# One DMA for each x, cond, bias and output tile, new orders of the five engines in the loading phase, and base loaded ahead of the recurrent LSTM weights

## What is computed

```python
ys = cond / sqrt(512);  d = rsqrt((ys*ys) @ (w0*w0) + 1e-8)
x = x + ((x * ys) @ w0) * d                                  # L0
h = tanh(h @ Wh1 + x @ Wx1 + b1), h0 = cond;    x = x + h    # L1, a recurrence over 128 steps
xw = gelu(layernorm(cond) @ w1 + b1) @ w2 + b2               # L2: cond alone gives a low-rank
layer = base + A @ B^T (A, B: two halves of xw, rank 8)      #     matrix for each sequence
x = x + x + x @ layer^T
gates = x @ Wx3 + h @ Wh3 + b3                               # L3, an LSTM over 128 steps
c = f*c + i*g;  h = o*tanh(c);                  x = x + h
```

## Time and profile before

| what | us |
|---|---|
| median of 3 runs | 1211.31 (1210.25 to 1211.34) |
| the profiled execution | 1212.77 |
| its span in the trace | 1211.0 |
| PE, DVE, ACT, POOL busy | 1149.9, 858.9, 480.3, 56.0 |

### The profile page before, as it was taken

The page is one execution under the profiler, slowest core; times in us unless marked ns, Lnnn a source line. Parts: engine busy times, 40 slices in busy tenths (PEclk is TensorE's granted clock), DMA queues, the critical chain, the costliest instruction groups (busy, mean ns, idle before and its releaser), DMA issues.

```text
span 1211.0 us, 50535 instructions
## 1 busy us (share of the span) xinstructions
PE 1149.9 (95%) x22740; PEld 751.8 (62%) x22740; DVE 858.9 (71%) x2389; ACT 480.3 (40%) x1160; POOL 56.0 (5%) x75
## 2 busy tenths in 40 slices
PE   3885999999999999999999999999999999999985
PEld 1562666666666666666666666666666666666542
DVE  4796777777777777777777777777777777776553
ACT  4694333333333343333333433333334333334332
POOL 1000000000000000000000000000000000000000
PEclk9888999999999999999999999999999999999999
DMA  9982000000000000000000000000000000000000
GB/s 321 390 302 67 3 20 21 20 21 20 20 15 8 20 20 21 20 20 20 11 12 20 20 20 21 20 21 11 12 20 20 21 20 20 11 8 6 11 11 18
DMA packets 49064, 50.99 MB, mean 42 GB/s; under 512 B 5984, under 2 KB 38752, under 8 KB 47184
## 3 DMA queue, kind: packets, MB, share of 16 engines
q1 hardware_dynamic: 47984, 47.50, 12.5%
q10 hardware_dynamic: 864, 0.26, 0.1%
HBM read 39.36 MB, written 8.39 MB: 39 GB/s over the span
## 4 chain that ended last, share of the span: by engine, by line
PE 63%; DVE 19%; ACT 11%; issue 4%; DMA 2%; ACTq 0%; DVEq 0%
PE ps_gates L1331 20%; PE ps_gates L1323 18%; PE ps_x L1262 7%; PE ps_l L1262 6%; PE ps_rnn L1347 4%; PE ps_rnn L1350 3%; ACT rows L476 2%; PE ps_lr L1262 2%; DVE gates_ring L998 2%; PE ps_z L1262 2%; DVE lstm_hT L1009 2%; ACT gates_ring L598 2%; DVE late L987 1%; DVE rnn_h L841 1%; ACT x L476 1%
## 5 line engine op out<-in xcount | busy, mean ns | idle before, releaser
L1331 PE MATMUL ps_gates<-big,lstm_h 128*32 128x512 f16 x6144 | 355.0, 380 | 9.9 <-ACT lstm_h L476 8.1
L1323 PE MATMUL ps_gates<-big,rows 128*32 128x512 f16 x6144 | 355.3, 380 | 3.5 <-DVE rows L742 3.5
L1323 PEld LDWEIGHTS ps_gates<-big,rows 128*32 128x32 f16 x6144 | 164.8, 97 | 171.8 <-issue 5.6
L1331 PEld LDWEIGHTS ps_gates<-big,lstm_h 128*32 128x32 f16 x6144 | 152.4, 96 | 163.4 <-ACT lstm_h L476 16.3
L998 DVE SCALAR_TENSOR_TENSOR gates_ring<-ps_gates,tile_un,rows 128x256 f32<-128x256 f32 x256 | 111.5, 477 | 42.0 <-PE ps_gates L1331 42.0
L598 ACT ACTIVATE gates_ring<-gates_ring 128x256 f32<-128x256 f32 x128 | 53.5, 418 | 199.7 <-DVE gates_ring L998 199.7
L1347 PEld LDWEIGHTS ps_rnn<-rnn_h,wh_hi 128*128 128x128 f16 x2048 | 90.4, 96 | 57.5 <-issue 52.6
L1347 PE MATMUL ps_rnn<-rnn_h,wh_hi 128*128 128x64 f16 x2048 | 120.5, 192 | 3.9 <-DVE rnn_h L841 3.9
L1350 PE MATMUL ps_rnn<-rnn_h,wh_lo 128*128 128x32 f16 x2048 | 116.1, 177 | 0.0
L476 ACT ACTIVATE lstm_h<-lstm_hT,tile_g 128x128 f16<-128x128 f32 x128 | 51.6, 403 | 120.4 <-DVE lstm_hT L1009 120.4
L1350 PEld LDWEIGHTS ps_rnn<-rnn_h,wh_lo 128*128 128x128 f16 x2048 | 90.8, 97 | 0.0
(11 more groups left out here) (180 smaller groups left out, 1552.2 us busy)
## 6 DMA issues: line engine op xcount, KB each, us to landing
ring<-in_hw SPq DMA_DIRECT2D x16, 1024.0 KB, 12.6
xT_sb<-in_xT SPq DMA_DIRECT2D x128, 64.0 KB, 2.3
outT<-late SPq DMA_DIRECT2D x128, 64.0 KB, 2.1
big<-in_wx SPq DMA_DIRECT2D x5, 1024.0 KB, 7.8
big<-in_wh SPq DMA_DIRECT2D x5, 1024.0 KB, 12.2
big<-in_w SPq DMA_DIRECT2D x1, 1024.0 KB, 5.8
big<-in_hw SPq DMA_DIRECT2D x1, 1024.0 KB, 11.8
late<-in_base SPq DMA_DIRECT2D x1, 1024.0 KB, 18.3
```

Of the source, the lines that this page charges most:

```text
L1323: nc.tensor.matmul(ps_gates[t % 2][B * j:B * j + B, :], x16[:, part, k, at:at + B], wx3_part(w_part, k)[:, GW * j:GW * j + GW], start=(n = ...
L1331: last = nc.tensor.matmul(ps_gates[t % 2][B * j:B * j + B, :], lstm_h16[:, part, k], wh3_part(w_part, k)[:, GW * j:GW * j + GW], start=Fal ...
```

## The change

1. x tiles, output tiles, condT and b1T are moved by one DMA each in place of four (`by_feature` in place of `by_block`). The partitions that hold the features stay the same. condT moves from ACT's queue to the head of SP's.
2. SP issues base behind blocks 4 to 7 of w2, ahead of the four parts of Wh3. The squares of base are taken before those of Wh3, and POOL's order follows.
3. The layer norm no longer waits for hb1T, which has a semaphore of its own.
4. The calls of the loading phase stand in another order on all five engines. ACT's tanh of a recurrence step and its `high` part may stand apart (`rnn_tanh`, `rnn_high`), and so may DVE's `x3_first` and `x3_low`. In the main loop the calls follow each other as before.

```diff
-        def by_block(x, j):
-            return x.rearrange("(f k) j n -> j f k n", k=KC)[j]
+        def by_feature(x):
+            return x.rearrange("(f k) j n -> j f k n", k=KC)
...
         def x_landed(engine, c):
-            engine.wait_ge(ld_x[c % XT_RING], 16 * KC * (c // XT_RING + 1))
+            engine.wait_ge(ld_x[c % XT_RING], 16 * (c // XT_RING + 1))
...
             def load_x(c):
-                for j in range(KC):
-                    sp.dma_start(xT_sb[c % XT_RING][FB * j:FB * j + FB].rearrange("p k t b -> p k (t b)"),
-                                 by_block(xT[c].rearrange("p j t b -> p j (t b)"), j)).then_inc(ld_x[c % XT_RING], 16)
+                sp.dma_start(xT_sb[c % XT_RING][:].rearrange("p k t b -> p k (t b)"),
+                             by_feature(xT[c].rearrange("p j t b -> p j (t b)"))).then_inc(ld_x[c % XT_RING], 16)
...
+            sp.dma_start(condT_sb[:], by_feature(condT)).then_inc(ld_cond, 16)
             load_weight(w0, W0_SLOT, ld_w0)
             load_x(0)
...
             for c in range(1, XT_RING):
                 load_x(c)
-            for j in range(KC):
-                sp.dma_start(b1T_sb[FB * j:FB * j + FB], b1T.rearrange("(f k) j -> j f k", k=KC)[j],
-                             allow_slow_non_contiguous=True).then_inc(ld_b1, 16)
+            sp.dma_start(b1T_sb[:], b1T.rearrange("(f k) j -> j f k", k=KC), allow_slow_non_contiguous=True).then_inc(ld_b1, 16)
             for k in range(KC):
                 sp.dma_start(wx3_staged(k), by_row(wx3)[:, k]).then_inc(ld_wx3[k], 16)
             for n in range(RING, 2 * RING):
                 sp.wait_ge(w2_used, n - RING + 1)
                 load_w2(n)
+            sp.dma_start(late[:].rearrange("p (k n) -> p k n", k=KC), by_row(base)).then_inc(ld_base, 16)
...
                 else:
                     sp.wait_ge(u_parts, 1)
                 sp.dma_start(wh3_staged(k), by_row(wh3)[:, k]).then_inc(ld_wh3[k], 16)
-            sp.dma_start(late[:].rearrange("p (k n) -> p k n", k=KC), by_row(base)).then_inc(ld_base, 16)
             for n in range(2 * RING, 4 * KC):
...
                 sp.wait_ge(out_ready, STEPS * (a + 1))
-                for j in range(KC):
-                    sp.dma_start(by_block(out[a].rearrange("p j t b -> p j (t b)"), j),
-                                 x3T[a % 2][FB * j:FB * j + FB].rearrange("p k t b -> p k (t b)"))\
-                      .then_inc(st_out[a % 2], 16)
+                sp.dma_start(by_feature(out[a].rearrange("p j t b -> p j (t b)")),
+                             x3T[a % 2].rearrange("p k t b -> p k (t b)")).then_inc(st_out[a % 2], 16)
             for q in range(2):
-                sp.wait_ge(st_out[q], 16 * KC * TILES // 2)
...
-            def rnn(r):
+            def rnn_tanh(r):
                 i, s = r // STEPS, r % STEPS
-                h = x2T[i % X2_RING][:, :, s]
                 act.wait_ge(rnn_pre_ready, r + 1)
                 if s == 0:
                     wait(act, x2_lo_ready, i - X2_RING + 1)
-                nc.scalar.activation(h, rnn_pre[:], ACT.Tanh).then_inc(rnn_h_ready, 1)
+                nc.scalar.activation(x2T[i % X2_RING][:, :, s], rnn_pre[:], ACT.Tanh).then_inc(rnn_h_ready, 1)
+
+            def rnn_high(r):
                 act.wait_ge(rnn_h_ready, r + 1)
-                high(rnn_h16[:, :, 0], h, s_h).then_inc(rnn_hi_ready, 1)
+                high(rnn_h16[:, :, 0], x2T[r // STEPS % X2_RING][:, :, r % STEPS], s_h).then_inc(rnn_hi_ready, 1)
+
+            def rnn(r):
+                rnn_tanh(r)
+                rnn_high(r)
 
...
-            for j in range(KC):
-                act.dma_start(condT_sb[FB * j:FB * j + FB], by_block(condT, j)).then_inc(ld_cond, 16)
             act.dma_start(ln_rows[:, 0], cond).then_inc(ld_rows, 16)
             act.dma_start(ln_rows[:, 1], ln_g.partition_broadcast(B)).then_inc(ld_rows, 16)
             act.dma_start(ln_rows[:, 2], ln_b.partition_broadcast(B)).then_inc(ld_rows, 16)
-            act.dma_start(hb1T_sb[:], hb1T).then_inc(ld_rows, 16)
-
+            act.dma_start(hb1T_sb[:], hb1T).then_inc(ld_hb1, 16)
+
+            act.wait_ge(ld_w0, 16)
+            squares(big[:, SQ_SLOT], big[:, W0_SLOT], 1)
             act.wait_ge(ln_var_ready, 1)
             nc.scalar.activation(ln_s[:, 1:2], ln_s[:, 0:1], ACT.Sqrt).then_inc(ln_root_ready, 1)
-            act.wait_ge(ld_w0, 16)
-            squares(big[:, SQ_SLOT], big[:, W0_SLOT], 1)
             act.wait_ge(ld_wx1, 16)
             unused_squares(big[:, WX1_SLOT], 2, 1)
...
+            rnn(5)
+
+            nc.scalar.activation(unused[:], s_h, ACT.Sigmoid)
+            copy_rows(2)
...
+            copy_rows(3)
+            rnn_tanh(7)
+            b_high()
             wh3_high(2, 0)
-            copy_rows(3)
             wh3_high(2, 1)
+            low_rank_share(0)
+            x3_high(0)
             wh3_high(3, 0)
-
-            nc.scalar.activation(unused[:], s_h, ACT.Sigmoid)
-            b_high()
...
-            def x3(a):
-                x3_flat = x3T[a % 2].rearrange("p k t b -> p (k t b)")
+            def x3_first(a):
                 dve.wait_ge(tile_un_ready, a + 1)
-                wait(dve, st_out[a % 2], 16 * KC * (a // 2))
+                wait(dve, st_out[a % 2], 16 * (a // 2))
                 dve.wait_ge(base_ps, a + 1)
                 dve.wait_ge(lr_ready, a + 1)
-                nc.vector.scalar_tensor_tensor(x3_flat, ps_x3[:], tile_un[:, a, 1:2], x3_lr, ALU.mult, ALU.add)\
-                  .then_inc(x3_ready, 1)
+                nc.vector.scalar_tensor_tensor(x3T[a % 2].rearrange("p k t b -> p (k t b)"), ps_x3[:], tile_un[:, a, 1:2], x3_lr,
+                                               ALU.mult, ALU.add).then_inc(x3_ready, 1)
+
+            def x3_low(a):
                 dve.wait_ge(x3_hi_ready, a + 1)
-                low(x3_16[a % 2][:, 1].rearrange("p k n -> p (k n)"), x3_flat, tile_g[:, a, 0:1],
-                    x3_16[a % 2][:, 0].rearrange("p k n -> p (k n)")).then_inc(x3_lo_ready, 1)
+                low(x3_16[a % 2][:, 1].rearrange("p k n -> p (k n)"), x3T[a % 2].rearrange("p k t b -> p (k t b)"),
+                    tile_g[:, a, 0:1], x3_16[a % 2][:, 0].rearrange("p k n -> p (k n)")).then_inc(x3_lo_ready, 1)
 
             def lstm_gates(t):
                 a, gates = t // STEPS, gates_sb[t % 2]
...
             nc.vector.tensor_scalar(ln_s[:, 0:1], moments[:, 1:2], LN_EPS, None, ALU.add).then_inc(ln_var_ready, 1)
             x_magnitude(0, 0)
+            xs(0)
...
+            wh1_low(0)
+            x_magnitude(1, 1)
             xs(1)
-            dve.wait_ge(ld_b1, 16 * KC)
+            x_magnitude(2, 2)
+            x_magnitude(3, 3)
+            x1_low(0)
...
             pe.wait_ge(folds_ready, 3)
+            pe.wait_ge(ys_ready, 2)
+            pe.wait_ge(sq_ready, 1)
+            folded_parts(ps_x3, ysq, w0_sq).then_inc(dsum_parts, 1)
             pe.wait_ge(ae_ready, 1)
             for k in range(KC):
...
             w2_unit(1)
             w2_unit(2)
+            w2_unit(3)
             pe.wait_ge(wx1_lo_ready, 2)
             l1(0)
-            w2_unit(3)
+            l0(1)
             pe.wait_ge(wh1_lo_ready, KC)
             pe.wait_ge(h0_lo, 1)
             rnn(0)
-            l0(1)
+            w2_unit(4)
             rnn(1)
-            w2_unit(4)
             w2_unit(5)
+            w2_unit(6)
             rnn(2)
+            w2_unit(7)
             l1(1)
+            turn_a()
             rnn(3)
-            w2_unit(6)
-            w2_unit(7)
             l0(2)
-            turn_a()
             rnn(4)
-            rnn(5)
-            l1(2)
             w2_unit(8)
             w2_unit(9)
+            rnn(5)
             w2_unit(10)
-            w2_unit(11)
             pe.wait_ge(a_lo_ready, 4)
             z(0)
+            w2_unit(11)
+            l1(2)
             rnn(6)
+            w2_unit(12)
+            w2_unit(13)
+            rnn(7)
+            w2_unit(14)
+            w2_unit(15)
+            move_b()
             pe.wait_ge(base_lo_ready, 2)
             x3_base(0, range(KC))
-            w2_unit(12)
-            w2_unit(13)
-            w2_unit(14)
-            rnn(7)
-            w2_unit(15)
-            move_b()
             pe.wait_ge(b_lo_ready, 2)
             x3_low_rank(0)
             pe.wait_ge(wx3_lo_ready, 2 * KC)
```

More of the change, by code:

```diff
@@ L660, in _ @@
+            wx3_high(2, 1)
+            copy_rows(1)
+            rnn(2)
+            base_squares()
+            wx3_high(3, 0)
+            wx3_high(3, 1)
+            rnn(3)
+            a_high()
             wh3_squares(0)
-            rnn(3)
-            copy_rows(1)
-            wx3_high(2, 0)
+            x2_high(0)
+            rnn(4)
+            base_high(0)
+            x1_high(2)
             wh3_squares(1)
             wh3_squares(2)
-            rnn(4)
-            x1_high(2)
             wh3_squares(3)
-            wx3_high(2, 1)
@@ L1058, in _ @@
             weight_scale(2, 3, wx1_scale_ready)
```

(82 more changed lines are left out.)

133 lines of the change are left out of this document (53 added, 80 removed).

## The result

| | before | after |
|---|---|---|
| time, median | 1210.78 us (1210.21 to 1211.34) | 1219.45 us (1218.12 to 1221.77) |
| profiled execution, its span | 1212.77, 1211.0 us | 1219.4, 1217.6 us |

The ratio is 1.0074, 95% interval 1.0056 to 1.0091: the change makes the kernel slower by 8.7 us. The forecast was 1218.9.

The account below looks back on a forecast made before the run. It took PE to bound the main loop and the last w2 block's landing plus a DMA-free chain the loading phase. Last block +6.8, chain -1.0 and tail +1.8 gave +7.6 on 1211.3: 1218.9 us, range 1202 to 1225.

Parts of the forecast that it names:

- Stall in the weight stream, -5.1: Loading phase: reordered w2 units free the four-place ring, removing the empty DMA stretch from 77.7 to 82.8 us; -5.1 us.
- Twelve x issues, -1.0: SP's queue in loading: three x issues in place of twelve stop the queue running dry; -1.0 us, bounds 0 and -2.
- The head, 0: Start of the kernel: earlier layer norm and one more ACT table load change nothing while DMAs set the pace; 0.
- Merging, +12.9: Loading phase: merged DMAs run over four engines and delay later weights; +12.9 us, bounds 0 and +17.
- condT's 1.6: Loading phase: condT's 128-byte packets on four engines cost 1.6 us more, the middle of 0 to 3.3.
- Last block, +6.8: End of the weight stream: the last w2 block lands at 104.1 us in place of 97.3, +6.8 us.
- Behind the last block, -1.0: Chain from the last w2 block to gates_x(0): b_high and b_low start earlier; -1.0 us, bounds +1.5 and -1.6.
- base ahead of Wh3, 0: Loading phase: base's DMA moved earlier arrives in time for DVE's base_diagonal; 0, bounds 0 and +2 us.
- Tail, +1.8: Kernel end: the single last output DMA over four engines lands later; +1.8 us, bounds -1.1 and +2.3.
- Sixteen engines: Rival for the merged DMAs: they are shared over all engines as before, -8.2 us, 1203.1 us; chance 0.22.
- Rival 2: Merged DMAs in between, as eight engines or cheaper packets: 1.1 us more a tile, 1206.8 us; chance 0.08.
- rival 3: Loading phase: late x tiles make DVE the bound, recurrence starting at 53 us, time 1219.7 us; chance 0.10.

Follow-up runs that it names:

- e1: The changed kernel with its new orders, but condT, x, b1T and output tiles each in four DMAs again: 1209.57 us, ratio 0.9999.
- e9: e1 with condT's four DMAs back at the head of ACT's queue: 1206.84 us, ratio 0.9963.
- e4: The changed kernel with x, cond, bias and output laid out by the host for one DMA each with 128 as outermost count: 1201.61 us, ratio 0.9933.
- e6: The kernel before, its orders kept, with the data layout and single DMAs of e4: 1206.43 us, ratio 0.9964.
- e2: The kernel before, its orders kept, with the merged DMAs alone: 1219.81 us, ratio 1.0088.
- e7: The changed kernel with x tiles alone in four DMAs again: 1211.92 us, ratio 1.0002.
- e8: e4 with GpSimd's product xs(3) moved ahead of its maximum of B: 1199.29 us, ratio 0.9896.
- e12: e8 with base's DMA moved back behind the four parts of Wh3: 1210.98 us, ratio 1.0002.

## Why the prediction came out, step by step

The time was right to 0.6 us and its main mechanism was right, but several sizes were wrong and cancelled, so that the number came out is in part luck. Of the signs that it named, the slow stretch came, but at 87 GB/s from 29 to 38 us where it had some 60 for 12; no stretch is empty ahead of the last block, PE waits 3.32 us for a DMA ahead of unit 8 and for DVE at most 0.8 us at a time on the way there, and the last block landed at 98.7, between its 104 and 91.

- **Stall in the weight stream, -5.1: right.** e1 against the kernel before moves 387 in place of 257 GB/s from 70 to 85 us: 1.95 MB or 5.0 us. At the last block the orders bring 4.3 us (e9) and, in the 128 form, 4.5 (e4 against e6).
- **Twelve x issues, -1.0: not had.** The ragged rates of the earlier trace rows were not a dry queue: the DMA share there is 1.25 from 28 to 30 us and 0.85 in the one us from 31. Three issues over four engines take SP longer than twelve. Only the 128 form has a gain, 407 (e4) against 340 GB/s (e1) from 27 to 42 us, or 2.6 us, and there fewer issues and longer runs are not told apart.
- **The head, 0: wrong.** condT's issues now stand ahead of all weights on SP. That costs e1 0.8 MB in the first 10 us, 2.1 us. Undoing it alone (e9) brings the last block 2.6 us earlier, the time by 4 us by the two ratios (2.3 between the profiled spans). The prediction weighed the layer norm's wait and the table load there, and put nothing down for what condT's place at the head of SP's list costs the weights behind it.
- **Merging, +12.9: mechanism right, size twice too large.** Measured 6.1 (after against e1) and 7.6 (e2 against before) at the last block, all of it by the x tiles (e7). I scaled a tile's time from 235 GB/s over sixteen engines to 59 over four, 4.5 us. Measured are 87 GB/s and 3.0 us. An engine of sixteen moves 15 GB/s of these packets and counts as fully busy (the share of 1.25), an engine of four moves 22. So the rate does not go with the number of engines; what the sixteen share that slows each packet was not tried. Of the 8.0 us that the stretch from 27 to 42 lost against e1 (207 GB/s over 15 us), 1.9 did not reach the last block (6.1 did), near the 2.3 taken. condT's 1.6 was nothing.
- **Last block, +6.8: measured +4.5**, as -4.3 from the orders (94.22 to 89.97), +2.6 from the head (to 92.61) and +6.1 from the merging (to 98.73).
- **Behind the last block, -1.0: measured +1.3, near its upper bound.** The earlier `b_low` is real: in e8 the chain is 12.45 us, 1.0 under 13.4. After the change, too, `b_low` starts 1.2 us behind the scale, where it was 2.3. But there two things cover it. `x3_low` took 1.76 us beside GpSimd's product; the prediction had not looked at GpSimd. And TensorE's granted clock was 0.50 (1.2 GHz) from 98.7 to 105.0, after PE had waited 2.15 us; unit 15 took 1.93 us there (1.07 before) and `move_b` 3.68. The wait alone doesn't decide it: in e8 PE had waited 2.19 us and the clock was 1.00. Nor does the program: `move_b` took 1.94 and 3.42 us in the two profiles of before. What decides was not found. Before, `move_b` at that clock (3.42 us in the second profile) lay beside the table load, and x3_base was done; now `x3_base(0)` stands behind it, and is on the path. Of the 2.2 us over e8's chain 1.0 is `x3_low`, 0.9 unit 15, and 0.3 `move_b` with `x3_base(0)` behind it, the rest of which lies beside DVE's own work. First `move_b` of before in the second profile and then the stretches: after the change, and in e8, where the clock is 1.00 (2.4 GHz):

```profile
96.00 3.42 PE L1254 MATMUL ps_l<-rows,half_ident 128*64 128x512 f32 x8 [0.72 <-ACT rows L542]
```

```profile
98.70:105.00 6.30, 5.55 (x16) 0.97 (x17) 3.19 (x12) 1.48 (x3) 1.33 (x1) 0.50 0.22 66
```

```profile
85.90:90.00 4.10, 3.33 (x23) 1.04 (x24) 2.28 (x4) 0.80 (x2) 1.29 (x1) 1.00 0.13 46
```

- **base ahead of Wh3, 0: right for the change as made, but only half a statement.** DVE waits 2 us for base at its new place. At the old place under the new orders it would have waited 11.8 (e12). So the new order of DVE rests on the move, though e12 gives its price only from above.
- **Tail, +1.8: measured +2.3**, its upper bound.
- **Main loop, 0: held.** The +0.5 is within what two profiles of before differ by (1095.8 and 1096.9).
- **Rivals.** Sixteen engines is excluded by the rates. Rival 2, cheaper packets, had part of the mechanism: a tile cost 1.9 us more (3.0 against 1.1), between its 1.1 and the forecast's 3.4. DVE as the bound did not happen after the change: step 0 of the recurrence started at 50.4 where rival 3 had 53, and the chain to the last block has no DVE in it. e12 shows what it looks like. With the merging at its measured +6.1 and the rest as forecast, the sum would have been -5.1 - 1.0 + 6.1 - 1.0 + 1.8 = +0.8, no change. The head, GpSimd's product and the slower stretch, all missed, and the x issues that brought nothing, made the number come out.

The best version here is e8, the new orders with one DMA each of 128 outermost and GpSimd's product early: 1199.29 us, 1% under the kernel before.

## What to carry to other kernels

Before you merge DMAs, look at the outermost count on the HBM side: four feature groups as the outermost loop keep four engines busy and hold up every later transfer of the queue, while a layout with 128 outermost gives one issue and the full rate. A rate measured over sixteen engines does not scale down with their number: 235 GB/s became 87 on four and not 59, though the sixteen counted as fully busy. And when a wait is taken off a chain, look at every engine that touches the instructions behind it: here GpSimd and PE's slower stretch were already lying beside it.
